# Summing seven of nine passes beside the scatter instead of five, with a running maximum per body

## The reference, cut to what matters

```python
h = node_features @ Wn + bn;  q = node_features @ Wq + bq;  k = ... ;  v = ...
eh = edge_features @ We + be
attn_in = jnp.concatenate([q[src], k[tgt], eh], axis=-1)
hmid = jax.nn.leaky_relu(attn_in @ A1 + b1, SLOPE)
scores = jax.nn.leaky_relu(hmid @ A2 + b2, SLOPE)
w = jax.nn.softmax(scores.mean(axis=-1), axis=0)
out = jax.ops.segment_sum(w[:, None] * v[tgt], src, num_segments=num_nodes)
y = h + out
return gamma * (y - mu) / jnp.sqrt(var + EPS) + beta      # and x is added outside
```

## Time and profile before

| what | us |
|---|---|
| median of 3 runs (6712.77 to 6752.65) | 6719.47 |
| span of the profiled execution | 5084.8 |
| what lies around that span in the median | 1634.7 |
| groups and scatter, to the last scatter | 151.9 to 4239.4 |
| after the last group's rows, to the last early score | about 4208 to 4258 |
| check, branch and the 200 units left | 4258 to about 4574 |
| maximum, exponentials, first loads | about 4574 to 4592 |
| last stage, 98 blocks | 4592 to 5078 |

### The profile page before, as it was taken

How to read it: one execution, slowest core, us unless ns; L and a number is a source line. 1 busy time by engine, 2 the same in 40 slices (tenths; PEclk the granted TensorE clock), 3 DMA queues, 4 the chain that set the end, 5 groups by cost and what they waited for, 6 DMA issues and landing times. The chain is left out here.

```text
span 5084.8 us, 136782 instructions
## 1 busy us (share of the span) xinstructions
PE 4453.7 (88%) x34924; PEld 3609.7 (71%) x35287; DVE 3986.4 (78%) x9657; ACT 2814.3 (55%) x7064; POOL 3197.2 (63%) x3381
## 2 busy tenths in 40 slices
PE   8655567888899999999999999999999987997887
PEld 3544455666688878888788878887888765777776
DVE  7655555777788888888888888888888774768998
ACT  5333333444466666666666666666666542446666
POOL 2677777777777777777777777777777772000110
PEclk9888888999999999999999999999999998999999
DMA  8888877888999988898888889988988765888888
GB/s 247 196 237 256 252 233 239 270 267 261 280 314 316 318 256 262 260 266 250 264 262 262 261 253 263 264 264 251 265 262 263 222 207 161 220 232 212 227 235 210
DMA packets 1938633, 1276.16 MB, mean 251 GB/s; under 512 B 637802, under 2 KB 1830929, under 8 KB 1938444
## 3 DMA queue, kind: packets, MB, share of 16 engines
q1 hardware_dynamic: 1768101, 831.59, 62.7%
q0 software_dynamic: 154752, 435.99, 23.1%
q10 hardware_dynamic: 15592, 6.41, 0.5%
HBM read 703.28 MB, written 570.23 MB: 250 GB/s over the span
## 5 line engine op out<-in xcount | busy, mean ns | idle before, releaser
L1272 POOL DMA_INDIRECT slots<-rows,slot_i x3224 | 3105.3, 963 | 992.2 <-issue 923.1
L1327 PE MATMUL ps_row<-win,mixed 128*128 128x256 f32 x5904 | 1535.6, 406 | 116.7 <-ACT rows L1419 114.9
L1327 PEld LDWEIGHTS ps_row<-win,mixed 128*128 128x128 f32 x5904 | 1119.0, 202 | 301.7 <-ACT rows L1419 134.4
L1419 ACT ACTIVATE rows<-ps_row 128x512 f32<-128x512 f32 x1476 | 889.5, 603 | 60.7 <-PE ps_row L1327 59.8
L1416 ACT ACTIVATE rows<-lo_all 128x8 f32 (+1 forms) x403 | 87.2, 216 | 1435.4 <-DMA slots<-rows,slot_i 1435.4
L1298 PE MATMUL ps_e<-ident,edges 128*128 128x128 f32 x3224 | 510.8, 283 | 263.1 <-ACT mixed L1408 171.3
L1298 PEld LDWEIGHTS ps_e<-ident,edges 128*128 128x128 f32 x3224 | 415.5, 146 | 427.4 <-ACT mixed L1408 181.1
L845 ACT ACTIVATE low<-ps_z 128x512 f32<-128x512 f32 (+1 forms) x882 | 528.2, 599 | 340.4 <-PE ps_z L774 160.5
L867 DVE TENSOR_TENSOR mid<-low,ps_z 128x512 f32<-128x512 f32 (+1 forms) x882 | 589.2, 668 | 125.9 <-ACT low L845 100.5
L774 PE MATMUL ps_z<-onehot,q_bits 128*128 128x512 bf16 (+1 forms) x2283 | 628.4, 376 | 19.5 <-DVE onehot L857 0.3
L1472 ACT ACTIVATE early_v<-early_v,early_weight 128x128 f32<-128x128 f32 x1960 | 600.0, 415 | 0.0
(11 more groups left out here) (217 smaller groups left out, 5716.5 us busy)
## 6 DMA issues: line engine op xcount, KB each, us to landing
u_rows<-slots SPq DMA_DIRECT2D x880, 258.0 KB, 3.2
early_v<-slots SPq DMA_DIRECT2D x490, 258.0 KB
edges<-edge_attr_dram SPq DMA_DIRECT2D x403, 256.0 KB
q_bits<-qb_tab SPq DMA_DIRECT2D x882, 96.0 KB, 3.0
slots<-no_row SPq DMA_DIRECT2D x98, 528.0 KB
slots<-rows,slot_i POOLq DMA_INDIRECT x3224
v_own<-slots SPq DMA_DIRECT2D x198, 258.0 KB, 3.4
slots<-no_row SPq DMA_DIRECT2D x98, 396.0 KB
```

What stands on the lines that cost most here:

```text
L1272: pool.indirect_dma_start(slots_tab[h], bass.IndirectOffsetOnAxis(slot_i[:, u, j:j + 1], 0), rows[:, u, j, :], None).then_inc(scattered[u] ...
L1327: last = pe.matmul(bank[:, j % 2, :], mixed[:, u % 2, j, :], win[:, u, :], start=True, stop=True)
L1419: nc.scalar.activation(rows[:, u, 2 * k:2 * k + 2, 0:2 * U0].rearrange("p j (a c) -> p j a c", a=2)[:, :, :, 0:D], row_bank(s, k).rearrang ...
```

## The change

Seven passes are summed beside the groups and two are left. One pair of blocks is summed in each step, from body LAG = 2 on without a gap until all 343 pairs are done (pass p begins as soon as its first units have scores). INSIDE grows to 686 = 7 * 98, and the steps run on after the last group: 8 steps with two units and a pair each, and 9 with a pair alone. The maximum is no longer one per pass but runs from body to body: `find_top` (three small DVE instructions), `spread_top` (a matmul with 4 columns), `set_top` (two), `raise_body` (three on ACT, two of them small). Each sum is rescaled by the ratio of the maximum now to that of the pass before. The masks of pass MASKED are added as its scores are taken.

The last stage has LATE = 2 units to a block, and `finish` is spread over two blocks. BLOCKS, PRELOADED's check and the factor `part_inv` (now one per body) follow. `load_values` and `add_beta` are not edited; LATE in them is now 2.

```diff
-SOONER = 5
+SOONER = 7
+LAG = 2
-SPOTS = 2 * LATE
+SPOTS = 8
-BLOCKS = 4
+BLOCKS = 8
-        AFTER = 12
+        AFTER = 16
...
             def pair_begun(i, j):
 
-                n = i - SUM_BODY
-                if not 0 <= n < SUM_BODIES * SOONER:
-                    return None
-                q, r = n // SUM_BODIES, n % SUM_BODIES
-                return (q, r, j) if j < (PAIRS if r < SUM_BODIES - 1 else 1) else None
+                n = i - LAG
+                return ((n * PAIRS + j) // NQ, n, j) if 0 <= n * PAIRS + j < ALL_PAIRS else None
...
             def event_of(i):
-
-                n = i + 1 - SUM_BODY
-                return n // SUM_BODIES if n % SUM_BODIES == 0 and 0 <= n < SUM_BODIES * SOONER else None
+                return i - 1 if 0 < i <= LAST_BODY + 1 else None
...
+                    def bank_free(s, q, n, j):
+
+                        pe.wait_ge(based, s if in_group(s, 0) else NG)
+                        if not in_group(s, 0):
+                            pe.wait_ge(early_added, pair_number(q, n, j))
+
+                    def spread_top(n):
+
+                        pe.wait_ge(top_made, n * 3 + 3)
+                        pe.matmul(ps_top, body_max[:, 0:1].to_broadcast([P, P]), ident[:, 0:P:32], start=True, stop=True,
+                                  skip_group_check=True).then_inc(top_sent, 1)
...
+                    def raise_body(n):
+
+                        act.wait_ge(top_set, n * 2 + 4)
+                        nc.scalar.mul(body_max[:, 2:3], run_top[:, bass.ds(n + 1, 1)], -1.0 / H).then_inc(early_ready, 1)
...
+                    def find_top(n):
+
+                        dve.wait_ge(o.scored, n + 1)
+                        dve.sem_inc(passed, 1)
+                        w = units_left(o, n) * UNIT
+                        nc.vector.tensor_reduce(body_top[:, 0, 0:1], score[:, bass.ds(n * (BODY * UNIT), w)], AX_X, ALU.max).then_inc(top_made, 1)
+                        dve.wait_ge(top_made, n * 3 + 1)
+                        nc.vector.transpose(body_top[:, 1, :], body_top[:, 0, :]).then_inc(top_made, 1)
+                        dve.wait_ge(top_made, n * 3 + 2)
+                        nc.vector.tensor_reduce(body_max[:, 0:1], body_top[:, 1, :], AX_X, ALU.max).then_inc(top_made, 1)
+
+                    def set_top(n):
+
+                        dve.wait_ge(top_sent, n + 1)
+                        nc.vector.tensor_reduce(body_max[:, 1:2], ps_top, AX_X, ALU.max).then_inc(top_set, 1)
+                        dve.wait_ge(top_set, n * 2 + 3)
+                        nc.vector.tensor_tensor(run_top[:, bass.ds(n + 1, 1)], body_max[:, 1:2], run_top[:, bass.ds(n, 1)], ALU.max).then_inc(top_set, 1)
...
-        BUNCHES = (1, 1, 2, 2)
+        BUNCHES = (1, 2)
...
                 def sum_step(i, k, all_wide):
                     if has(i, k + LEAD):
                         place(*unit_at(i, k + LEAD))
...
-                    if has(i, k) and past(i, k - LATE):
-                        for part_of in ((), (1, 2), (3,), (4, 5))[k % LATE]:
-                            finish(i * BLOCKS + (k // LATE - 1), (k // LATE - 1) % 2, part_of)
+                    if has(i, k):
+                        for back, part_of in (((2, 4), (2, 5), (1, 1), (1, 2)), ((1, 3),))[k % LATE]:
+                            if past(i, k - back * LATE):
+                                finish(i * BLOCKS + (k // LATE - back), (k // LATE - back) % 2, part_of)
                     if k % LATE == LATE - 1 and has(i, k):
                         add_part(i * BLOCKS + k // LATE, i, all_wide)
```

More of the change, by code:

```diff
@@ L1048, in steady @@
             def steady(eng, first, end, step):
-                n = first - SUM_BODY
-                q = n // SUM_BODIES if 0 <= n < SUM_BODIES * SOONER else None
+                here = pair_begun(first, 0)
+                scaled[0] = first - 1 >= FIRST_RATIO
+                mask_now[0] = masked(first)
                 with eng.Fori(first, end) as i:
@@ L1054, in steady @@
                         begun_here = closed_here = None
[L1055 to L1063, removed]
+                        if here is not None:
+                            begun_here = (here[0], i - LAG, j)
+                            closed_here = (here[0], i - LAG, j - 1) if j else (here[0], i - (LAG + 1), UNROLL - 1)
+                        step(i * UNROLL + (START + j), j, [(i, 2 * j), (i, 2 * j + 1)], begun_here, closed_here, first > AT_CUT, i - 1)
             def one_body(i, step):
+                mask_now[0] = masked(i)
+                scaled[0] = i - 1 >= FIRST_RATIO
                 for j in range(UNROLL):
                     s = i * UNROLL + START + j
[L1069 to L1077, removed]
+                    if s < END:
+                        units = [(i, k) for k in (2 * j, 2 * j + 1) if i * BODY + k < INSIDE]
+                        step(s, j, units, pair_begun(i, j), pair_closed(i, j), s + 1 >= CUT, event_of(i))
             def both_steps(eng, step, stops=None):
@@ L1082, in both_steps @@
                 stops = {} if stops is None else stops
[L1083 to L1086, removed]
+                alone = {0, AT_CUT} | {i for i in range(STEADY) if not uniform(i)}
+                marks = {i for i in alone} | {i + 1 for i in alone} | set(stops) | {STEADY, MASK_FROM + 1, MASK_END + 1, FIRST_RATIO + 1}
+                marks = sorted(i for i in marks if i <= STEADY)
                 for at, after in zip(marks, marks[1:]):
@@ L1093, in both_steps @@
                         steady(eng, at, after, step)
-                last_body(step)
+                for i in range(STEADY, END_BODY + 1):
+                    one_body(i, step)
             with nc.Block() as block:
@@ L1259, in _ @@
                         load(NG, NG % UNROLL)
-                        for g in range(INSIDE - AFTER, INSIDE):
-                            unit(g, g % RING, g - NT * (DONE - 1), DONE - 1)
+                        for t in range(NG, END):
+                            for g in range(2 * (t - START), min(2 * (t - START) + 2, INSIDE)):
+                                unit(g, g % RING, g - NT * (DONE - 1), DONE - 1)
+                            early = pair_begun((t - START) // UNROLL, (t - START) % UNROLL)
+                            if early is not None:
+                                load_early(*early)
                 @block.gpsimd
@@ L1474, in weigh_early, with both @@
                         op.then_inc(early_weighed, 1)
-                    def both(s, u, units, begin, close, second):
+                    def both(s, u, units, begin, close, second, event):
                         late = len(units) // 2
-                        event = event_of((s - START) // UNROLL) if known(s) and u == 3 else None
-                        copy_rows(s, u, 0)
+                        if in_group(s, 0):
+                            copy_rows(s, u, 0)
                         if in_group(s, 1):
@@ L1727, in spot_early, with both @@
                         op.then_inc(early_spotted, 1)
-                    def both(s, u, units, begin, close, second):
-                        event = event_of((s - START) // UNROLL) if known(s) and u == 1 else None
+                    def both(s, u, units, begin, close, second, event):
+                        set_here = event if u == 2 else None
                         if in_group(s, 2):
                             one_hot(s + 2, (u + 2) % UNROLL)
-                        unit(*units[0])
+                        for n in units[:1]:
+                            unit(*n)
                         if in_group(s, 2):
@@ L1815, in score_steps @@
             border = SHORT_FROM // o.units
[L1816 removed]
+            assert 2 < border < LEFT - 3 and SHORT_FROM - border * o.units <= o.units - BATCH
             for k in range(o.units):
@@ L1819, in score_steps @@
             short_units[0] = False
-            with eng.Fori(1, border) as i:
+            with eng.Fori(1, border - 1) as i:
                 for k in range(o.units):
                     step(i, k)
-            for k in range(o.units):
-                step(border, k)
+            for i in (border - 1, border):
+                for k in range(o.units):
+                    step(i, k)
             short_units[0] = True
```

324 lines of the change are left out of this document (178 added, 146 removed).

## The result

| | us |
|---|---|
| before, median of 4 runs (6684.62 to 6752.65) | 6716.12 |
| after, median of 4 runs (6835.81 to 6884.25) | 6843.05 |
| after / before | 1.0188, 95% interval [1.0139, 1.0237] |
| predicted | 6887, range 6805 to 6980 |

What follows compares the result with a forecast made beforehand. POOL's scatter was taken to bound the groups, DVE the last stage before the change and a circle through SP after it. 6719.5 us plus 168 (0 + 54 - 7 + 121) gave 6887 us, range 6805 to 6980.

Steps and rivals of the forecast that it cites:

- the circle of one block: Last stage: o_sb, add_beta, SP's x, then v, back to o_sb in series, 5.94 us a block, 6.65 with part_in; +121 us.
- The load of 193.5 KB: Last stage: a unit's v load, taken as 3.0 us from issue to use; the skill's rule would give about 2.45.
- The rival of DVE's pace: Last stage: loads of v run further ahead, 3.24 us a block, stage 318 us, total 6599 us; chance 0.07.
- The tail: After the last group: 8 steps at 8 us, 9 pairs alone at 4.5, 104 us against 50; +54, between +33 and +80.
- The left units: Units left after the sums beside the groups: four fewer at 1.6 us each, -7 us.
- Beside the groups: Groups: 98 more pairs and the running maximum are covered by POOL's scatter; 0 us, up to 30 for the range.
- such gaps: Groups: POOL gaps waiting for ACT's rows would mean that the slack beside the groups was not there.
- the 1634.7 us: Time around the profiled span of 5084.8 us, left as it is by the change.

Runs made afterwards that it cites:

- second trace of before: The kernel before, unchanged, run and traced again: 6725.01 us, ratio 1.0006; its traced execution had a span of 6765.1 us.
- experiment 6: The changed kernel with four buffers of x and three quarters of each early sum's matmuls left out: 6555.11 us, 0.9724 of before.
- experiment 7: The changed kernel with four buffers of x and four reductions instead of one in find_top: 6587.96 us, 0.9767 of before.
- experiment 2: The changed kernel with four buffers of x in place of two: 6608.86 us, 0.9811 of before.
- experiment 8: The changed kernel with four buffers of x in place of two, run once more: 6574.22 us, 0.9762 of before.

## Why the prediction was right

**The last stage, the circle of one block.** Predicted 607 us against 486, +121; measured 596.1 against 484.6, +111.5. The links, predicted and measured: o_sb to xb 0.49 and 0.43; xb to x 0.65 and 0.68; x to v 0.95 and 1.12; v to its use 3.0 and 2.84; place to o_sb 0.85 and 0.80; sum 5.94 and 5.87. With `part_in` 6.65 and 6.59. It is shown from three sides that this is the cause: two more buffers, a shorter lead, and another place for x in SP's queue each take 195 to 275 us off the stage (first to last o_sb), and no load was made shorter or smaller. Four buffers give 3.23 us a block, the 3.24 that the forecast had for the work alone.

**The load of 193.5 KB.** 2.84 us from issue to use in the block above, and 2.7 from issue to landing in the median of the stage. The Trainium skill's sum (DMA: Bandwidth & Descriptors, Anatomy of one DMA) gives about 2.45 us for it, as an estimate. It is a fit to DMAs that GpSimd issues, and these loads are issued by SyncE, a difference that the prediction passes over; it is 0.25 to 0.4 us too low here, and 0.4 beside the 3.01 us of the earlier trace rows. The Trainium skill's rule to issue early and wait late (the same page, Rules for kernel authors) is what the experiments bear out: all three ways of more distance between issue and use paid.

**The rival of DVE's pace** (6599 us) did not come, but it was priced well: once the circle is open the kernel takes 6609 and 6574.

**The tail.** Predicted 104 us where there were 50, +54. From the last `base` to the check it is 126.6 us now, +47.8 to the second trace of before and +64.0 to the first, from which the 50 were read. Steps took 7.1 us where I took 8, pairs alone 5.2 where I took 4.5, so two errors partly cancel. The bounds of +33 and +80 do not follow from their terms either: 8 * 7.1 + 9 * 4.0 and 8 * 9.3 + 9 * 5.9 give +43 and +78.

**The left units.** -7 predicted, -7.3 measured.

**Beside the groups.** That 98 more pairs and the running maximum cost nothing fits the stages (5716 and 5641), and experiments 6 and 7 test it: neither three quarters of the matmuls less nor a longer chain moves the time by anything like its own length, and the groups by nothing that can be told from their scatter. So the term of 0 was right. But the reason that I gave was wrong for the executions that count, and as far as my reason goes it was luck that the 0 held. I read from the earlier trace rows that the scatter bounds the groups at 1.26 us, with 0.9 us of slack on PE in a step of 10.1. In the timed executions a step of after is 5641 / 402 = 14.0 us and a scatter's share 1.75, POOL stands idle for ACT's rows (1186.7 us over the span), and PE is busy 238.7 of 300 us in the stretch shown. The first sums on PE came at 1140 us and not at 930, which fits the slower pace. I named such gaps as what would show that the slack was not there. They are there, but they are in the second trace of before as well (1123.2 us), and by experiment 6 PE has slack. The page after has them in this line:

```profile
L1283 POOL DMA_INDIRECT slots<-rows,slot_i x3224 | 3097.9, 961 | 2573.7 <-ACT rows L1441 1186.7
```

**The sum.** I added differences (54 - 7 + 121 = 168) to the median, and the span that I could not explain I left as it was. The differences come from stages in which both traces of before agree, to 0.6 and 1.1 us in the last two. That is why 6887 came within 44 us of 6843, and not because the 1634.7 us were understood. The stages after the groups alone add up to +152, near my 168; the medians differ by 127, and the 41 us between are within what the groups of one kernel differ by from one execution to the next (48 us in experiments 2 and 8). The step that failed is "what lies around the span": it is the groups, which take 5716 us and not 4050.

## What to carry to other kernels

Where a stage has fewer steps to a block, count again in blocks what every wait and buffer was worth in steps. A wait that stood seven steps behind its cause stood one step behind after this change, and a load behind it in the same queue then sets the pace. It is cured at whichever link is cheapest: two more buffers, or the small load behind the large one. And a span that is far from the run's time is to be explained before a bound is read from it; price changes as differences between stages that hold in more than one execution.

## What the runs showed of the hardware that was not expected

One program, two paces: 238 scatters in 300 us in the first trace, 156 to 175 in this stretch in the others. In the slower pace the same instructions are no longer than in the first trace (a scatter 0.96 us, a copy of rows 0.60), but PE, ACT and DVE stand still, again and again, for some us. The tables of waits tell the two apart. In the first trace the largest wait in the groups is ACT's for the scatter (2000 to 3600 us), and from 200 to 4000 us no engine has a wait for the releaser that the profile calls remote. In the second trace of before such waits are among the largest (2000 to 5400 us):

```profile
ACT rows L1416 <- DMA slots<-rows,slot_i: 558.7, 158, 5.8
```

```profile
ACT low L845 <- remote: 911.1, 154, 9.6
...
DVE onehot L857 <- remote: 501.3, 118, 8.3
...
ACT rows L1419 <- remote: 283.2, 105, 7.4
```

The timeline of ACT in the changed kernel, ahead of all scoring, shows one such break:

```profile
304.97 0.20 ACT L1438 ACTIVATE rows<-lo_all 128x8 f32<-128x8 uint8 x1
316.23 0.60 ACT L1441 ACTIVATE rows<-ps_row 128x512 f32<-128x512 f32 x1 [11.06 <-remote]
```

The wait for the scatter of four groups earlier stands ahead of the first of the two, so it was over by 304.97, and PE's matmuls for the second were done by 305.07 by the profile. DVE is idle from 308 to 323 and PE from 307 to 317 us, and POOL works off the scatters that it has. PE's granted clock falls with the idle time (0.86 in the stretch of the earlier trace rows, where it had been 1.00). I have no experiment that shows what releases them. It is not the load that the early sums put on PE: the break shown comes 835 us before the first of them, and the groups are as long without three quarters of them (experiment 6). The cause stays open.

In the last stage of the changed kernel, with DVE waiting for loads and PE for DVE, PE's granted clock is 0.59 on average, between its two levels of 1.2 and 2.4 GHz, and a matmul of 128 columns takes 0.42 us; with four buffers the clock is 0.96 and such a matmul 0.28 to 0.30. PE is not in the circle: no instruction of DVE waits for it in that stage, so it costs nothing here.
